# Attention weights turned by the vector engine and DRAM instead of by the matrix engine, with layer norm 2 moved to the scalar engine, in a three-layer graph network

## The reference

```python
h = jnp.maximum(_layernorm(x, axis=-1), 0.0)
# then, for l in range(3), with x = h at first
si = x @ attn_w[l, :d]
sj = x @ attn_w[l, d:]
scores = si[:, :, None] + sj[:, None, :] + attn_b[l]
scores = jnp.where(scores >= 0, scores, 0.2 * scores)
scores = jnp.where(mask, scores, -jnp.inf)
attn = jax.nn.softmax(scores, axis=-1)
agg = jnp.einsum('bij,bjd->bid', attn, x)
h = layernorm(x + agg, g1[l], beta1[l])
ff = jax.nn.gelu(h @ W1[l] + b1[l], approximate=False) @ W2[l] + b2[l]
x = layernorm(h + ff, g2[l], beta2[l])
```

## Time and profile before

| | |
|---|---|
| median of 3 runs | 1242.56 us (1242.36 to 1243.44) |
| the profiled execution | 1241.6 us, its span 1239.8 us |
| granted TensorE clock | 0.998 of full |
| PE busy | 1196.4 us, 97% |
| DVE busy | 1075.9 us, 87% |
| ACT busy | 920.0 us, 74% |
| POOL busy | 677.4 us, 55% |
| chain that ended last | PE 95%, DVE 3%, SP queue 1%, DMA 1% |

### The profile page before, as it was taken

The page is one execution under the profiler, slowest core; times in us unless marked ns, Lnnn a source line. Parts: engine busy times, 40 slices in busy tenths (PEclk is TensorE's granted clock), DMA queues, the critical chain, the costliest instruction groups (busy, mean ns, idle before and its releaser), DMA issues.

```text
span 1239.8 us, 23072 instructions
## 1 busy us (share of the span) xinstructions
PE 1196.4 (97%) x7509; PEld 1082.8 (87%) x7509; DVE 1075.9 (87%) x3568; ACT 920.0 (74%) x1754; POOL 677.4 (55%) x648
## 2 busy tenths in 40 slices
PE   2699999999999999999999999999999999999997
PEld 1589999998999999999999999999999999999996
DVE  5899889999998888899998888899989988888865
ACT  3786887678877776778778767777887777677752
POOL 1354455456755554456666545554666455545564
PEclk9999999999999999999999999999999999999999
DMA  7122322233332111222432122122432321122221
GB/s 256 38 77 73 99 70 60 77 94 112 103 103 88 50 44 52 85 71 85 129 114 92 43 59 70 44 69 78 125 115 80 100 60 43 44 69 61 78 89 48
DMA packets 109620, 100.57 MB, mean 81 GB/s; under 512 B 12952, under 2 KB 95932, under 8 KB 109500
## 3 DMA queue, kind: packets, MB, share of 16 engines
q1 hardware_dynamic: 109500, 99.10, 26.3%
HBM read 66.47 MB, written 32.60 MB: 80 GB/s over the span
## 4 chain that ended last, share of the span: by engine, by line
PE 95%; DVE 3%; SPq 1%; DMA 1%; issue 0%; POOL 0%; ACT 0%; DVEq 0%; POOLq 0%
PE acc L1073 44%; PE hbank L1058 42%; PE mix L1087 7%; PE mix L1112 2%; DMA adji<-in_adj_dram 1%; DVE xs L757 0%; DVE junk L694 0%; DVE st L603 0%; DVE st L764 0%; SPq L313 0%; PE util L1104 0%; SPq L332 0%; DVE sc L729 0%; POOL rstd L467 0%; DVE hid_lo L615 0%
## 5 line engine op out<-in xcount | busy, mean ns | idle before, releaser
L1073 PE MATMUL acc<-w2hi,hid_hi 128*128 128x256 f32 x1536 | 442.2, 288 | 0.0
L1073 PE MATMUL acc<-w2hi,hid_lo 128*128 128x256 f32 x1536 | 434.5, 283 | 0.0
L1073 PE MATMUL acc<-w2lo,hid_hi 128*128 128x256 f32 x1536 | 434.4, 283 | 0.0
L912 ACT ACTIVATE hbank<-hbank,vec 128x512 f32<-128x512 f32 x384 | 255.4, 665 | 178.1 <-PE hbank L1058 167.0
L1058 PE MATMUL hbank<-ht_hi,w1hi 128*128 128x512 f32 x768 | 305.7, 398 | 3.6 <-DVE hid_lo L615 2.0
L1058 PE MATMUL hbank<-ht_lo,w1hi 128*128 128x512 f32 x768 | 300.7, 392 | 0.0
L1073 PEld LDWEIGHTS acc<-w2lo,hid_hi 128*128 128x128 f32 x1536 | 294.0, 191 | 6.9
L1073 PEld LDWEIGHTS acc<-w2hi,hid_hi 128*128 128x128 f32 x1536 | 293.9, 191 | 6.9
L1058 PE MATMUL hbank<-ht_hi,w1lo 128*128 128x512 f32 x768 | 299.3, 390 | 0.0
L615 DVE TENSOR_TENSOR hid_lo<-hbank,hid_hi 128x512 fp32r<-128x512 f32 x384 | 259.9, 677 | 39.4 <-ACT hid_hi L918 39.4
L1073 PEld LDWEIGHTS acc<-w2hi,hid_lo 128*128 128x128 f32 x1536 | 293.9, 191 | 0.0
(11 more groups left out here) (80 smaller groups left out, 1708.4 us busy)
## 6 DMA issues: line engine op xcount, KB each, us to landing
z_dram<-tz SPq DMA_DIRECT2D x46, 512.0 KB, 2.6
zt<-z_dram SPq DMA_DIRECT2D x184, 128.0 KB, 2.8
sj_bc<-sj_dram SPq DMA_DIRECT2D x47, 256.0 KB, 3.9
xraw<-in_x_dram SPq DMA_DIRECT2D x16, 512.0 KB, 4.1
out_dram<-xout SPq DMA_DIRECT2D x32, 256.0 KB, 3.0
xres<-in_x_dram SPq DMA_DIRECT2D x15, 512.0 KB, 5.0
xout<-in_L_gnn_W_dram SPq DMA_DIRECT2D x10, 512.0 KB, 5.5
adji<-in_adj_dram SPq DMA_DIRECT2D x16, 256.0 KB, 3.5
```

The source lines that it names most:

```text
L912: act.activation(hbank[k % HB][:], hbank[k % HB][:], ACT.Gelu, bias=b1c(i.l, c)).then_inc(gelu_n, 1)
L1073: mm = pe.matmul(to, v[:, k % HID, of_g], w[:, i.l, c], start=c == 0 and n == 0 and g % HG == 0, stop=c == C - 1 and n == 2, skip_group_ch ...
```

## The change

It has five parts. E of items 2 and on is turned like z: VectorE turns 32x32 blocks into `te` (its output has a stride of four elements between neighbours), `send_e` writes them to DRAM and four DMAs of `move_e` bring them to `ET`, whose layout is now (block, i, graph), so that `aggregate` reads each graph's stationary operand with a stride of four elements. The first two items are still turned by TensorE, now through `util`. Second, `j_dots`/`i_dots` of layers 1 and 2 read x after `norm2` and before gamma and beta; `fold_attn`, run once in the first such `j_dots`, multiplies the attention rows by gamma and adds the beta part to the bias; `x_gamma` therefore waits for `i_dots` of item q+4. Third, `norm2` moves to ScalarE (Identity with scale and bias), and a small VectorE instruction `shift2` makes its bias. Fourth, `minus_max` becomes one VectorE instruction, and ScalarE makes `negm` by Prelu. Fifth, the lists of all engines are reordered, `residual` is at the end of the slot of its own item, the start is reordered, and inputs and adjacencies of items 1 and 2 get places of their own (in `hb`, `zt` and `tz`), so that they load without waiting.

```diff
-EARLY = 1
+EARLY = 2
+        early = [hb[:, 0], zt[:].rearrange("p m a g t -> p (m a g t)").rearrange("p (g d) -> p g d", g=GG)]
+        early_adj = tz[:].bitcast(I32).rearrange("p c g t -> p (c g t)").rearrange("p (i g j) -> p i g j", i=EARLY, g=GG)
...
+            def send_e(i):
+                sp.wait_ge(te_n, moved(i.q))
+                wait(sp, et_in, MOVES * (moved(i.q) - 1))
+                sp.dma_start(e_dram, te[:].rearrange("p b t g -> p (b t g)")).then_inc(e_sent, 16)
+            def move_e(i):
+                sp.wait_ge(e_sent, 16 * moved(i.q))
+                sp.wait_ge(agg_n, 2 * i.q)
+                for b in range(NQ):
+                    sp.dma_start(ET[b * QD:(b + 1) * QD].rearrange("p a t g -> p a (t g)"),
+                                 e_dram.rearrange("(a p) (b f) -> b p a f", a=NQ, b=NQ)[b]).then_inc(et_in, 16)
...
 x_gamma (pool)
+                if i.l < L - 1:
+                    pool.wait_ge(dots_n, i.q + BATCH + 1)
...
 (dve) norm2 becomes
+            def shift2(i):
+                dve.wait_ge(rstd_n["2"], i.q + 1)
+                dve.scalar_tensor_tensor(out=nmr2[:], in0=mv["2"][:, :, 0], scalar=-1.0, in1=rstd["2"][:],
+                                         op0=ALU.mult, op1=ALU.mult).then_inc(nmr2_n, 1)
...
+            def fold_attn():
+                dve.wait_ge(attn_rest_in, 16)
+                dve.wait_ge(ln2_in, 16 * 2)
+                for l in range(1, L):
+                    gamma, beta = ln2_rows[:, 0, l - 1], ln2_rows[:, 1, l - 1]
+                    dve.tensor_tensor_reduce(junk[:, 0], beta, attn_rows[:, l, 0], 1.0, attn_bias[:, l:l + 1],
+                                             ALU.mult, ALU.add, attn_part[:, l:l + 1]).then_inc(attn_fold_n, 1)
+                    dve.wait_ge(attn_fold_n, done)
+                    dve.tensor_tensor_reduce(junk[:, 0], beta, attn_rows[:, l, 1], 1.0, attn_part[:, l:l + 1],
+                                             ALU.mult, ALU.add, attn_bias[:, l:l + 1]).then_inc(attn_fold_n, 1)
+                    dve.wait_ge(attn_fold_n, done)
+                    dve.tensor_tensor(attn_rows[:, l], attn_rows[:, l], gamma.unsqueeze(1).to_broadcast([P, 2, D]),
+                                      ALU.mult).then_inc(attn_fold_n, 1)
...
 minus_max (dve)
-                dve.scalar_tensor_tensor(out=below[:, :, 0], in0=msj[:, :, 0], scalar=-1.0, in1=si_of(i), op0=ALU.mult,
-                                         op1=ALU.subtract).then_inc(below_n, 1)
-                dve.scalar_tensor_tensor(out=negm[:], in0=below[:, :, 0], scalar=SLOPE, in1=below[:, :, 0], op0=ALU.mult,
-                                         op1=ALU.min).then_inc(negm_n, 1)
+                dve.tensor_tensor_reduce(below[:, :, 0], msj[:, :, 0], si_of(i), 1.0, 0.0, ALU.add, ALU.max,
+                                         below_max).then_inc(below_n, 1)
+            def turn_e(i):
+                dve.wait_ge(exp_n, GG * (i.q + 1))
+                dve.transpose(te[:].rearrange("p b i g -> p b g i"), sc[:].rearrange("p g (b j) -> p b g j", j=QD)).then_inc(te_n, 1)
...
 (act)
+            def norm2(i, h):
+                act.wait_ge(nmr2_n, i.q + 1)
+                for g in range(h * HG, (h + 1) * HG):
+                    act.activation(y2_of(i)[:, g], y2_of(i)[:, g], ACT.Identity, bias=nmr2[:, g:g + 1],
+                                   scale=rstd["2"][:, g:g + 1]).then_inc(z2_n, 1)
 exps
+                act.wait_ge(below_n, i.q + 1)
+                act.activation(negm[:], below[:, :, 0], ACT.Prelu, scale=-SLOPE, alpha=1 / SLOPE).then_inc(negm_n, 1)
...
 aggregate (pe)
+                    if i.q < BY_PE:
+                        pe.wait_ge(eto_n, i.q + 1)
+                    else:
+                        pe.wait_ge(et_in, MOVES * moved(i.q))
-                    turned = ET[:, g]
+                    turned = ET[:].rearrange("p a i g -> p (a i) g")[:, :, g]
```

More of the change, by code:

```diff
@@ L780, in slot @@
                 t, f, b, a, d, p, n = item(s - 1), item(s), item(s + 1), item(s + 2), item(s + 3), item(s + 4), item(s + 5)
-                if t:
-                    residual(t, 0)
-                if a:
-                    minus_max(a)
-                if t:
-                    residual(t, 1)
+                if b:
+                    turn_z(b)
+                if f:
+                    low(f, 1)
+                if a:
+                    turn_e(a)
+                if t:
                     moments2(t)
@@ L799, in slot @@
                 if t:
-                    norm2(t, 1)
+                    shift2(t)
+                if f:
+                    low(f, 4)
+                split_weights(s + 5)
+                if d:
+                    j_dots(d)
+                if p and p.l == 0:
+                    input_moments(p)
+                if d:
+                    i_dots(d)
+                if p and p.l == 0:
+                    input_shift(p)
+                if b:
+                    h_low(b, 0)
                 if a:
@@ L803, in slot @@
                 if f:
[L804 to L806 removed]
+                    low(f, 5)
                 if a:
@@ L833, in slot @@
                 if b:
-                    low(b, 1)
+                    low(b, 0)
+                if a:
+                    norm1(a)
+                if d:
+                    minus_max(d)
+                if f:
+                    residual(f, 0)
+                    residual(f, 1)
             i0, i1, i2, i3 = (item(q) for q in range(0, 4))
             input_moments(i0)
+            turn_vectors()
+            penalty(i0)
             input_shift(i0)
-            penalty(i0)
-            turn_vectors()
+            penalty(i1)
             j_dots(i0)
@@ L862, in _ @@
             norm1(i0)
+            input_moments(i3)
             h_low(i0, 0)
             attend(i1, 0)
[L865 removed]
+            masked(i2)
             h_low(i0, 1)
             attend(i1, 1)
[L868 removed]
+            i_dots(i2)
             moments1(i1)
+            split_weights(3)
             minus_max(i2)
[L871 removed]
+            penalty(i3)
             low(i0, 0)
+            input_shift(i3)
             norm1(i1)
[L874 removed]
+            turn_e(i2)
             low(i0, 1)
+            split_weights(4)
+            j_dots(i3)
             low(i0, 2)
[L877 to L878 removed]
             low(i0, 3)
+            split_weights(5)
+            low(i0, 4)
+            low(i0, 5)
+            h_low(i1, 0)
+            i_dots(i3)
+            low(i0, 6)
             attend(i2, 0)
[L881 removed]
+            masked(i3)
             attend(i2, 1)
[L883 removed]
+            h_low(i1, 1)
             moments1(i2)
[L885 to L888 removed]
+            minus_max(i3)
             low(i0, 7)
[L890 removed]
+            low(i1, 0)
             norm1(i2)
[L892 to L896 removed]
+            residual(i0, 0)
+            residual(i0, 1)
             for s in range(1, ITEMS + 3):
@@ L1098, in z1_turn @@
             def z1_turn(i, m):
-                wait(pe, htlo_n, KD * i.q + m)
-                if i.q == 0 and m == 0:
-                    pe.wait_ge(mask_n, 1)
+                wait_util_read()
+                read["z"] += 1
                 for g in range(GG):
```

330 lines of the change are left out of this document (168 added, 162 removed).

## The result

| | before | after |
|---|---|---|
| median | 1242.46 us | 1234.01 us (1233.53 to 1234.50, 4 runs) |
| profiled execution | 1241.6 us | 1233.53 us, span 1231.7 us |

The ratio is 0.9931, with a 95% interval of 0.9919 to 0.9944: 8.5 us faster, where 23.2 were forecast. The sign holds and the four transposes are gone as forecast; the size does not hold, since the strided weight loads, priced at 0, took back 10.4 us. The time is just at the upper edge of the range (1234).

The account below looks back on a forecast made before the run. TensorE's own work was taken to bound the steady part, with TensorE waiting in the start. 19.8 + 1.9 + 4.7 - 1.85 - 1.3 = 23.2 off 1241.6 gives 1218.4, plus 1.0: 1219.4 us; range 1213 to 1234.

Parts of the forecast that it names:

- The stride of E ... I take 0: Aggregation's weight loads at 16 bytes between neighbours: bounds 0 and 13 us lost, 0 taken because loads hide beside matmuls.
- rival C: Slower: strided loads outgrow their cover in the aggregation; 0.063 us a piece eats all 23.2, 0.11 gives 1260; chance 0.09.
- The start, 4.7: Before slot 1: earlier adjacency brings h_low(i0,1) to 39.8, 6.6 gained less 1.9 later; 4.7 us, bounds 0 and 7.
- the walk of +34.3: In the start, TensorE walked from h_low(i0,1) reaches slot 1 34.3 us later, where before it took 32.4.
- e_turn and the wait for et_out: TensorE's steady slots: 45 x 0.44 = 19.8 us of transposes go, 38 x 0.05 = 1.9 us of waits; slot 24.21.
- the walk of the loop in a light slot: Aggregation through VectorE's row, Exp, turn_e and low f2 to ffn1 f5: low f2 at 5.2, needed 5.62, slack 0.4 us.
- 3 x 0.4 = 1.3 us lost: First slot of a round with input moments, one in twelve: low f5 done at 16.1, not 15.7; 1.3 us lost.
- fold_attn: Slot 1, once: 3.6 us on VectorE make low f5 end at 17.6, wanted 15.77; 1.85 us lost.
- The end: After the last ffn2 the order is kept: 0 gained.
- A (the loop binds): Loop from aggregation to ffn1 f5 is 0.25 to 0.5 us too long every slot: 1231 to 1242; chance 0.22.
- D (E's DMAs late): No change: ET lands at 13.1 instead of 11.0, each slot waits 0.5, 23 us gone, 1242; chance 0.05.
- B: The start gives nothing because weights and later x share the DMA queues: 1224; counted within the forecast's 0.62.

Follow-up runs that it names:

- E contiguous: Changed kernel with E put in place by four sends and ET brought back contiguous by four DMAs of 32 partitions: 1231.88 us, ratio 0.9918.
- the filled pause: Changed kernel with 26 extra matmuls of 128x256, adding no result, in TensorE's pause in the start: 1233.45 us, ratio 0.9921.
- the fastest but one: Changed kernel with early Exp, four sends and four returns of E, and E in pairs 8 bytes apart: 1225.32 us, ratio 0.9863.
- the first kernel with E contiguous: Changed kernel with E put in place by four sends and ET brought back contiguous by one DMA: 1300.58 us, ratio 1.0474.
- the one with the early Exp: Changed kernel with ET contiguous by four DMAs, plus a single-column Exp ahead of ScalarE's wait for minus_max: 1230.01 us, ratio 0.9893.

## Why the prediction was wrong

By its own steps, on the profiled executions (8.1 us gained, 23.2 forecast, 15.1 missing; each is a single execution, so tenths of a microsecond are not firm):

- **"The stride of E ... I take 0"** is the step that failed. The load grew by a factor of 1.68, and I had argued that a factor of 2 would hide in a piece of 0.216. It did not: the eight pieces went from 1.73 to 1.96, 0.029 each, 0.23 a slot, 45 x 0.23 = 10.4 us. I had no reason to prefer the lower bound: that a transpose gets load and matmul into 0.11 says nothing of a load that reads otherwise, and the trace of before had the aggregation's own loads, at 195 ns. The upper bound, 0.03 a piece, was nearly exact (8 x 46 x 0.03 is 11 us; the 13 of the prediction needs 0.034). That is partly luck. It added 0.14 for the stride from the mean of `masked`, 419 ns, but the median of those 188 is 382, and the mean is raised by eight that took 665 to 1483. With the median, 0.11 + 0.10 = 0.21 would have said that the load hides. This is rival C's mechanism below its point of decision (0.063); C's own price was off, since it had 0.11 a piece for a load of 0.33, and a load of 0.327 cost 0.029. The Trainium skill's page "SBUF — State Buffer" (the note on 16-byte cachelines) had warned of just this edit, and puts the limit of a free stride at four fp32; the runs here find 8 bytes free and the 16 bytes between neighbours of this change not.
- **The start, 4.7, measured 1.7.** Of the 3.0 missing, 2.4 are there when `h_low(i0,1)` is done: 42.24, forecast 39.8. `norm1(i0)` began at 33.00, about 0.7 later than forecast, and took 2.32 instead of 1.4 us, partly beside GpSimd. From its start `h_low(i0,1)` took 9.24 us, where E contiguous and the filled pause, both at a clock of 1.00 there, took 8.47 and 8.49: about 0.75 is the first stretch of slow clock. `et_out` for the first two items takes 1068 ns instead of 590, since it writes with the stride, but with E contiguous `norm1(i0)` began no earlier (33.28), so it explains nothing here. Behind that point the walk of +34.3 measured 77.15 - 42.24 = +34.9. The execution with the filled pause, which has neither slow stretch, began slot 1 at 77.3, so the clock costs the start nothing in the end; what would be the next thing to shorten is open.
- **e_turn and the wait for et_out** are right: without the stride the light slot is 24.22, forecast 24.21. So is the walk of the loop in a light slot: no wait of TensorE there with its 0.4 us of slack.
- **Long slots: "3 x 0.4 = 1.3 us lost"** (the product is 1.2) was too small. The profile of after shows them about 0.2 longer each, 3.2 us in all with one of 25.42. I had found only the first of each round, and had given the small VectorE instructions the time they have when they run alone.
- **fold_attn**: 1.25 us of wait, forecast 1.85. **The end**: nothing, as forecast.
- Together: 10.4 + 3.0 + 1.9 - 0.6 = 14.7 of the 15.1.

Of the rivals, A (the loop binds) is true in the long slots only, and was hidden by the stride: with the loads mended it took back 8.8 of 10.4 us. D (E's DMAs late) is true there too, once E is sent in small pieces. B is near the measured gain of the start in its number only: it let nothing land earlier, and the adjacency did.

## What to carry to other kernels

Price a strided stationary operand by a run of its own before it goes into a full engine: here a quarter of a microsecond per slot ate nearly half the forecast gain, and pairs (8 bytes apart) had the benefit of a strided layout for nothing. When one of several loops is shortened by 1%, look for the next one in the heaviest slots and not in the average: the busy share of TensorE was 97% before and after, and 96% in the fastest but one. Where ScalarE waits for a small result ahead of a change of function, let it load the table during the wait.

## What the runs showed of the hardware that I had not expected

- A VectorE instruction that reads two operands in SBUF while a GpSimd instruction runs can take that one's whole length. `input_shift` on 4 elements per partition, 223 ns on average before, takes 1.23 us as GpSimd's multiplication (1.27) begins:

```profile
311.54 1.27 POOL L550 TENSOR_TENSOR xout<-xout,ln_rows 128x512 f32<-128x512 f32 x1
311.59 1.23 DVE L661 SCALAR_TENSOR_TENSOR nmr<-mv,rstd 128x4 f32<-128x4 f32 x1
```

  The Trainium skill's page "SBUF — State Buffer" tells of a port pair shared by VectorE and GpSimd that one holds for a whole instruction; by that rule, the rows agree: VectorE's instruction ends at 312.82, GpSimd's at 312.81. Which instruction is hit depends on timing: with `input_shift` off VectorE, `masked` took 1.48 instead of 0.38.
- An fp32 weight load of 128 columns: 195 ns contiguous, 202 at 8 bytes, 327 at 16. A VectorE transpose of 128x512 with its output 16 bytes apart takes 1120 ns, contiguous 700.
- One DMA that brings `ET` back, 256 KB, took 4.9 to 6.7 us from issue to landing; four of 64 KB, 32 partitions each, land in 2.1 each. It is not the size alone, since the changed kernel's send of E has 256 KB and 128 partitions too:

```profile
e_dram<-te SPq DMA_DIRECT2D x46, 256.0 KB, 2.0
```

  The slow one reads DRAM with an outer loop of 4, each of the four with one of 32. What of this costs the time was not tried.
- A pause of TensorE at the same place, 3.15 to 3.17 us long, saw the granted clock fall to 0.50 in some executions (the changed kernel) and stay at 1.00 in others (the first kernel with E contiguous, and the one with the early Exp). Before, it stayed at 1.00 through 12.73 us.
